# A gated linear attention block on one core: x's statistics, x's low half and the weight splits in another order, and one bank of k's transposes copied by VectorE

## The chip, the cores and the metric

The kernel runs on one core of a Trainium2 chip. The metric is the device time of one execution in microseconds (us), as a median of several runs; lower is better.

## The reference

Four sequences of 2048 tokens of 512 elements pass through two residual layers, all in float32:

```python
q = elu(LN(x) @ Wq) + 1;  k = elu(LN(x) @ Wk) + 1;  v = LN(x) @ Wv      # 16 heads of 64
a = sigmoid(LN(x) @ Wa + ba + 2.0)                                       # one decay per token and head
S = a * S + k (outer) v;   z = a * z + k                                 # for each head, token by token
x = x + ((q @ S) / (q @ z + 1e-6)) @ Wo
x = x + (LN(x) @ CB.T) * (SCB / 127) + bias
```

## The kernel before

The 8192 tokens are 64 chunks of 128 (NC = 64). The first phase computes the projections and the recurrence and stores the attention's rows in memory; the second phase (`step2`) applies Wo and the second layer. The change is in the first phase alone.

Every engine runs its own program: `steps` calls `step(i, pair, b)` for each chunk i, with pair = i // 2 and b = i % 2. Steps -1 to 3 and 60 to 65 are written out, those between are a loop over pairs. The order within an engine is the order of the calls in `step`, written by hand; between engines there are only semaphores, whose counts are values like "16 per load and pair" (`counts` gives a table: `x16[d]` is 16 (pair + d + 1)). A wait blocks everything behind it on its engine.

x is kept transposed for two chunks at a time (`xT_in`) and is split into a high and a low half, `xT_hi` by ScalarE and `xT_lo` by VectorE; each product is three passes, high by high, high by low and low by high. The weights are split in the same way, once, at the start: `split_hi(n)` and `split_lo(n)`, in six slabs n in the order of `order`, each when its load has landed and before the unit that needs it.

A step of TensorE begins with small matmuls: `transposes` of k into the two banks of SC, the carried part of the attention (`carried`), the state's update (`delta`, into DS), the part within a chunk (`within`) and the `scores` (into SC again, once k's transposes have been copied to `kT`). Group r = 1 is the upper half of the heads and runs one chunk behind group 0. Then come the units: products of 12 matmuls of 512 columns (k1, v1, k0, v0) and of 24 of 256 (q units). In a step with b = 1 the order is k1, v1, k0, q0, q1, v0, and `gate_logits` for the next pair runs before `within(0)`; with b = 0 it is k1, v1, q2, q3, k0, v0. k0, v0, q0 and q1 belong to the next chunk or pair.

VectorE has the elementwise work of both groups: `weighted_v`, `state`, `normalised`, `masked`, `scaled_q`, the sums `elu_k` and `elu_q`, the scans of `decay_matrix`, and for a pair `logit_sums`, `decays` and the statistics of x (`x_stats`, `x_moments`). ScalarE evacuates the banks. GpSimd raises the variance to the power -1/2 and normalises `xT_in` for the next pair (`x4`, L593 and L597) after SyncE has spread the moments over the partitions through memory (`spread_norm`).

SyncE issues all DMAs. In a step with b = 1 its order is: spread the decays of group 1, store attn of group 1, `store_decays` (waits for `decays()`), spread the decays of group 0, spread the products, store attn of group 0, and last `load_pair`, which is this (L461 to L466):

```python
for s in range(2):
    later = row(sp, i + 3 + s)
    sp.wait_ge(stats_ready, pairs[1])
    ...
    sp.dma_start(xt[s][:, :], x_rows[bass.ds(later, C), :]).then_inc(x_loaded[s], 16)
```

xt holds the rows of which `x_stats` takes the statistics. Pair 0's rows are loaded at the start, those of pair p + 2 in the step with b = 1 of pair p. In the kernel before, the step with b = 0 of pair p reads the rows of pair p + 1.

Of the kernel before, what the change touches and what calls it, by code (L numbers as in the profile page):

```python
# [5 lines left out]
def gated_linear_attention_block(  # L6
# [50 lines left out]
    GH = 4  # L57
# [59 lines left out]
    with ExitStack() as ctx:  # L117
# [498 lines left out]
        def _(act):  # L616
# [14 lines left out]
            for s in range(2):  # L631
                first_x_hi(s)

# [17 lines left out]
            def step(i, pair, b):  # L651
# [75 lines left out]
                if exists(i) or exists(i - 1):  # L727
                    copy_kT()
                if exists(i - 2):
                    copy_num(1)  # L730
                if exists(i - 1):
                    copy_num(0)
                if b == 1 and exists(i + 1):
                    exp_logits()
                    if not first:
                        act.wait_ge(xT_normal, pairs[0])
                        act.wait_ge(v_unit_ready[1], one[-1])
                        act.wait_ge(q_unit_ready[3], pairs[0])
                        x_hi(0)
                if second:  # L740
                    split_hi(3)
                if exists(i):
                    k1_parts()
                    if second:
                        split_hi(4)
                    copy_v(1)
                if b == 1:
                    if exists(i + 1):
                        if not first:
                            x_hi(1)  # L750
                        k0_parts()
                        if first:
                            split_hi(1)
                        q_parts(0)
                        if first:
                            split_hi(2)
                        chunk_decay()
                        q_parts(1)
                        copy_v(0)
                    elif exists(i):  # L760
                        chunk_decay()
                        rows_hi(1, 0)
                elif exists(i):
                    if second:
                        split_hi(5)
                    q_parts(2)
                    chunk_decay()
                    q_parts(3)
                    k0_parts()
                    copy_v(0)  # L770
# [21 lines left out]
        def _(dve):  # L792
# [50 lines left out]
            for s in range(2):  # L843
                x_lo(s, 1, tiles_of(xT_bank(s)))

# [41 lines left out]
            def step(i, pair, b):  # L887
                one = counts(dve, i, 1, (-3, -2, -1, 0, 1))
                pairs = counts(dve, pair, 1, (-1, 0, 1))
                x16 = counts(dve, pair, 16, (-1, 1))  # L890
# [124 lines left out]
                if gates:  # L1015
                    logit_sums()
# [5 lines left out]
                if gates:  # L1022
                    decays()
                    if not first:
                        x_lo(0, pairs[1], xT_in[:, :, tokens(0)])
                if normal:
                    x_stats(x16[1])
                if exists(i - 1):
                    if normal:
                        dve.wait_ge(stats_ready, pairs[1])  # L1030
                        wait(dve, norm_stored, x16[-1])
                    normalised(0)
                elif normal:
                    dve.wait_ge(stats_ready, pairs[1])
                if normal:
                    x_moments(pairs[1])
                if isinstance(i, int) and i == NC - 1:
                    output_weights_lo(1)
                if second:
                    split_lo(3)  # L1040
                if exists(i):
                    elu_k(1, 0)
                    if second:
                        split_lo(4)
                    if gates:
                        x_lo(1, pairs[1], xT_in[:, :, tokens(1)])
                    decay_matrix(1)
                    weighted_v(1, one[0], one[-1], o)
                if gates:
                    elu_k(0, 1)  # L1050
                    if first:
                        split_lo(1)
                    elu_q(0, 0)
                    if first:
                        split_lo(2)
                    elu_q(1, 1)
                elif exists(i + 1):
                    if second:
                        split_lo(5)
                    elu_q(2, 1)  # L1060
                    elu_q(3, 0)
                    elu_k(0, 1)
                if exists(i + 1):
                    decay_matrix(0)
# [39 lines left out]
        def _(pe):  # L1104
# [52 lines left out]
            first_due = {"k transposed": FIRST + 1, "gates": FIRST // 2 + 1}  # L1157
            for r in range(2):
                first_due[f"carried{r}"] = FIRST - r
                first_due[f"within{r}"] = FIRST - r  # L1160
                first_due[f"delta{r}"] = FIRST + 1 - r
                first_due[f"scores{r}"] = FIRST + 1
# [7 lines left out]
            def step(i, pair, b):  # L1170
# [66 lines left out]
                def carried(r):  # L1237

                    count = due(f"carried{r}", one[-1 - r])
                    pe.wait_ge(qs_ready[r], one[-1 - r])  # L1240
                    if r == 1:
                        wait(pe, num_copied[0], one[-2])
                    elif exists(i - 2):
                        pe.wait_ge(num_copied[1], one[-2])
                    pe.wait_ge(mid_ready[r], count)
                    begin(f"carried{r}")
                    for j in range(GH):
                        for e in range(2):
                            for a in range(2):
                                ps = slice(64 * e, 64 * e + 64)  # L1250
                                made = nc.tensor.matmul(num_of(a, e, j), qs[ps, GH * r + j, L * a:L * a + L],
                                                        (S_mid if a else S[o])[ps, GH * r + j, :],
                                                        start=(j == 0), stop=False)
                    made.then_inc(inter_ready[r], 1)

                def within(r):

                    count = due(f"within{r}", one[-1 - r])
                    pe.wait_ge(M_ready[r], one[-1 - r])
# [11 lines left out]
                def delta(r):  # L1271

                    count = due(f"delta{r}", one[0 - r])
                    if r == 1:
                        wait(pe, state_ready[0], one[-1])
                        if b == 0 and exists(i + 1):
                            pe.wait_ge(logits_ready, pairs[0])
                    elif exists(i - 1):
                        pe.wait_ge(state_ready[1], one[-1])
                    pe.wait_ge(vw_ready[r], count)  # L1280
                    begin(f"delta{r}")
# [10 lines left out]
                def scores():  # L1292

                    for r in (1, 0):
                        if exists(i - r):
                            count = due(f"scores{r}", one[0])
                            for u in range(2 * r, 2 * r + 2):
                                pe.wait_ge(q_ready[u], pairs[-1] if r == 1 and b == 0 else pairs[0])
                            pe.wait_ge(kT_copied[0], one[0])
                            pe.wait_ge(kT_copied[1], count)  # L1300
                            begin(f"scores{r}")
# [74 lines left out]
                if b == 1 and exists(i + 1):  # L1376
                    gate_logits()
# [6 lines left out]
                if b == 1 and exists(i + 1):  # L1384
                    k0_unit()
                    wait(pe, v_ready[1], one[0])
# [93 lines left out]
```

## Time and profile before

| | |
|---|---|
| time, median of 3 runs | 2191.49 us (2190.68 to 2196.81) |
| the profiled execution's own time | 2204.02 us |
| its span | 2202.2 us |
| TensorE matmuls (PE) | 2064.2 us, 94% |
| TensorE weight loads (PEld) | 1773.7 us, 81% |
| VectorE (DVE) | 1497.7 us, 68% |
| ScalarE (ACT) | 677.4 us, 31% |
| GpSimd (POOL) | 340.1 us, 15% |
| mean granted clock of TensorE | 0.988 |

The weight loads overlap the matmuls. A busy TensorE is not one at its peak: the ends of pipelined matmuls are modelled, so a start-to-start distance says more than a duration. The first phase takes about the first 1450 us. Times in the rows are from the span's start.

### The profile page before, as it was taken

To read this page: it belongs to the slowest core of one execution; us is meant where nothing else is said; L and a number is where in the kernel's file an instruction comes from. 1 tells how busy PE (TensorE), PEld (TensorE's weight loads), DVE (VectorE), ACT (ScalarE), POOL (GpSimd) and SP (SyncE) were. 2 spreads that over 40 slices of the span, in tenths; PEclk is the share of its full clock that TensorE was granted. 3 is DMA by queue.
4 is the path that set the end of the run, shared out by engine and by line. 5 is a ranking of instruction groups with operands and counts; after the bars stand their busy time and mean duration, and the time that the engine had idled before them with its cause. 6 is when DMAs were issued, how large, how long until landed. Compare 5 with 4: busy or idle time off the path is not lost. (4 is left out here: it accounts for less than half of the span.)

```text
span 2202.2 us, 71551 instructions
## 1 busy us (share of the span) xinstructions
PE 2064.2 (94%) x28424; PEld 1773.7 (81%) x28424; DVE 1497.7 (68%) x3308; ACT 677.4 (31%) x1288; POOL 340.1 (15%) x367
## 2 busy tenths in 40 slices
PE   4789999999999999999999999999889999999998
PEld 3677888888888888888888888888768888888887
DVE  5566767777767777777776777776755555555555
ACT  3333333333333333333333333333321111111111
POOL 1111122111113111112211112211000000000000
PEclk8899999999999999999999999999999999999999
DMA  5132332333332333333233333324423333333332
GB/s 178 43 95 84 96 96 82 87 98 113 94 94 86 86 91 107 100 96 91 86 85 105 108 91 96 86 82 131 124 99 114 114 114 111 113 114 111 111 110 88
DMA packets 204592, 220.81 MB, mean 100 GB/s; under 512 B 31360, under 2 KB 146560, under 8 KB 204544
## 3 DMA queue, kind: packets, MB, share of 16 engines
q1 hardware_dynamic: 204544, 220.13, 32.7%
q8 instruction: 35, 0.57, 0.1%
q14 instruction: 13, 0.11, 0.0%
HBM read 168.59 MB, written 51.44 MB: 100 GB/s over the span
## 5 line engine op out<-in xcount | busy, mean ns | idle before, releaser
L1189 PE MATMUL G<-w_hi,xT_hi 128*128 128x512 f32 x1024 | 414.2, 404 | 55.2 <-DVE xT_lo L817 39.2
L1189 PE MATMUL G<-w_lo,xT_hi 128*128 128x512 f32 x1024 | 404.0, 395 | 0.0
L1189 PE MATMUL G<-w_hi,xT_lo 128*128 128x512 f32 x1024 | 401.9, 392 | 0.0
L1189 PE MATMUL G<-xT_hi,w_hi 128*128 128x256 f32 x1024 | 292.0, 285 | 8.3 <-DVE w_lo L824 8.3
L1189 PE MATMUL G<-xT_hi,w_lo 128*128 128x256 f32 x1024 | 292.0, 285 | 0.0
L1189 PE MATMUL G<-xT_lo,w_hi 128*128 128x256 f32 x1024 | 291.9, 285 | 0.0
L681 ACT ACTIVATE relu_t<-G 128x512 f32<-128x512 f32 x256 | 152.8, 597 | 450.7 <-PE G L1189 450.7
L1189 PEld LDWEIGHTS G<-w_hi,xT_hi 128*128 128x128 f32 x1024 | 194.6, 190 | 109.5 <-issue 68.5
L906 DVE SCALAR_TENSOR_TENSOR qT<-exp_t,relu_t 128x512 f32<-128x512 f32 x128 | 88.9, 695 | 257.3 <-ACT exp_t L682 257.3
L1189 PEld LDWEIGHTS G<-w_hi,xT_lo 128*128 128x128 f32 x1024 | 194.6, 190 | 42.8
L1189 PEld LDWEIGHTS G<-w_lo,xT_hi 128*128 128x128 f32 x1024 | 195.0, 190 | 35.3
L1146 PE MATMUL DS<-w_hi 128*128 128x512 f32 x512 | 207.7, 406 | 6.3 <-DVE w_lo L861 6.3
L1189 PEld LDWEIGHTS G<-xT_hi,w_hi 128*128 128x128 f32 x1024 | 198.7, 194 | 11.6 <-issue 9.2
L1146 PE MATMUL DS<-w_lo,w_hi 128*128 128x512 f32 x512 | 200.9, 392 | 0.0
L1189 PEld LDWEIGHTS G<-xT_hi,w_lo 128*128 128x128 f32 x1024 | 198.7, 194 | 2.4
L1146 PE MATMUL DS<-w_hi,w_lo 128*128 128x512 f32 x512 | 200.2, 391 | 0.0
L1189 PEld LDWEIGHTS G<-xT_lo,w_hi 128*128 128x128 f32 x1024 | 198.6, 194 | 0.0
L578 POOL TENSOR_TENSOR moments<-vareps,minus_half 128x2 f32<-128x2 f32 x32 | 33.7, 1052 | 1031.7 <-DVE vareps L805 1031.7
L785 ACT ACTIVATE w_hi<-SC 128x512 fp32r<-128x512 f32 x64 | 38.3, 599 | 494.8 <-PE SC L1134 494.8
L999 DVE TENSOR_TENSOR_SCAN D<-abc,eye 128x512 f32<-128x512 f32 x128 | 176.5, 1379 | 0.0
L593 POOL TENSOR_TENSOR xT_in<-xT_in,bias_b 128x256 f32<-128x256 f32 x124 | 137.4, 1141 | 190.3 <-DMA bias_b<-norm_rows 190.3
L670 ACT ACTIVATE num_sb<-NUM 128x520 f32<-128x520 f32 x128 | 77.4, 605 | 251.1 <-PE NUM L1266 251.1
(131 smaller groups left out, 3757.2 us busy)
## 6 DMA issues: line engine op xcount, KB each, us to landing
abc<-decay_rows SPq DMA_DIRECT2D x256, 128.0 KB, 3.0
pbc<-product_rows SPq DMA_DIRECT2D x256, 128.0 KB, 3.1
attn_rows<-attn SPq DMA_DIRECT2D x512, 64.0 KB, 2.0
at_rows<-attn_rows SPq DMA_DIRECT2D x64, 512.0 KB, 3.3
xt<-in_x SPq DMA_DIRECT2D x64, 256.0 KB, 2.7
x_in<-in_x SPq DMA_DIRECT2D x64, 256.0 KB, 3.4
out_rows<-xt SPq DMA_DIRECT2D x64, 256.0 KB, 2.0
xT_in<-in_xT SPq DMA_DIRECT2D x31, 512.0 KB
```

The costliest lines, as they stand in the source:

```text
L578: pool.tensor_tensor(moments[:, :, 1], vareps[:, :], minus_half[:, :], ALU.pow).then_inc(rstd_ready, 1)
L593: made = pool.tensor_tensor(x4[:, kt, :, :], x4[:, kt, :, :], norm_b[:, 0, :, :], ALU.subtract)
L670: act.activation(num_sb[r][:, :, :, :], num_banks, ACT.Copy).then_inc(num_copied[r], 1)
L681: act.activation(relu_t[buffer][:, :], bank[:, :], ACT.Relu)
L785: act.activation(by_stretch(fT_hi), both_of(TF), ACT.Copy).then_inc(fT_hi_ready, 1)
L906: nc.vector.scalar_tensor_tensor(qT[:, QT * u:QT * u + QT, :].rearrange("p k c -> p (k c)"), exp_t[buffer][:, :], 1.0, relu_t[buffer][:, : ...
L999: nc.vector.tensor_tensor_scan(D[:, hs(r), :].rearrange("p h c -> p (h c)"), abc[:, HH * L * r:HH * L * (r + 1)], eye8[:, :, :].rearrange( ...
L1146: made = nc.tensor.matmul(to, a[:, kt, :], w[:, kt, :], start=(kt == 0 and n == 0), stop=(kt == tiles_k - 1 and n == 2))
L1189: made = nc.tensor.matmul(to, lhs, rhs, start=(n == 0), stop=(n == len(passes) - 1))
```

## The change

- Splits: slab 1 is split right behind slab 0, and slabs 2 to 5 each one place earlier in the first two steps.
- ScalarE copies only the first bank of k's transposes; VectorE copies the second as the first thing in its step.
- ScalarE: for the next pair, `x_hi(0)` goes ahead of `copy_num(0)`, and `exp_logits` behind it.
- VectorE, b = 1: `x_lo(0)` goes ahead of `decays()`; `decay_matrix(0)` ahead of `elu_q(1, 1)`; `x_stats` and `x_moments` move here from the step with b = 0, and read the rows of pair p + 2. With b = 0, `decay_matrix(0)` goes ahead of `elu_q(3, 0)`. The second pair's statistics (step 0) go behind `elu_q(2, 1)`.
- TensorE: waits of `carried`, `within`, `delta(1)` and `scores` are gathered ahead of `transposes`, and `scores` waits once for both groups. In step -1 `gate_logits` follows the first k unit.
- SyncE's and GpSimd's programs are as before.

```diff
 split_hi(0)
 for s in range(2):
     first_x_hi(s)
+split_hi(1)
...
-                    for a in range(2):
-                        act.activation(kT[:, held, stretch(a)], turned_k[a][:, held, :], ACT.Copy)\
-                            .then_inc(kT_copied[a], 1)
+                    act.activation(kT[:, held, stretch(0)], turned_k[0][:, held, :], ACT.Copy).then_inc(kT_copied[0], 1)
...
+                if gates and not first:
+                    act.wait_ge(xT_normal, pairs[0])
+                    act.wait_ge(v_unit_ready[1], one[-1])
+                    act.wait_ge(q_unit_ready[3], pairs[0])
+                    x_hi(0)
                 if exists(i - 1):
                     copy_num(0)
-                if b == 1 and exists(i + 1):
+                if second:
+                    split_hi(4)
+                if gates and not first:
                     exp_logits()
...
-                normal = b == 0 and exists(i + 2)
-
+                normal = b == 1 and exists(i + 3) and not first
+
+                if exists(i) or exists(i - 1):
+                    held = slice(0 if exists(i) else GH, PT if exists(i - 1) else GH)
+                    dve.wait_ge(kT_ready, one[0])
+                    nc.vector.tensor_scalar(kT[:, held, stretch(1)], turned_k[1][:, held, :], 1.0, None, ALU.mult)\
+                        .then_inc(kT_copied[1], 1)
...
-                if gates:
+                if gates and not first:
+                    x_lo(0, pairs[1], xT_in[:, :, tokens(0)])
                     decays()
-                    if not first:
-                        x_lo(0, pairs[1], xT_in[:, :, tokens(0)])
-                if normal:
-                    x_stats(x16[1])
...
                     elu_q(0, 0)
                     if first:
-                        split_lo(2)
+                        split_lo(3)
+                    decay_matrix(0)
+                    if normal:
+                        x_stats(x16[2])
+                        dve.wait_ge(stats_ready, pairs[2])
+                        dve.wait_ge(norm_stored, x16[0])
                     elu_q(1, 1)
+                    if normal:
+                        x_moments(pairs[2])
                 elif exists(i + 1):
+                    elu_q(2, 1)
+                    decay_matrix(0)
                     if second:
-                        split_lo(5)
-                    elu_q(2, 1)
+                        x_stats(x16[1])
+                        dve.wait_ge(stats_ready, pairs[1])
                     elu_q(3, 0)
+                    if second:
+                        x_moments(pairs[1])
                     elu_k(0, 1)
-                if exists(i + 1):
-                    decay_matrix(0)
...
                 def transposes():
 
                     count = due("k transposed", one[0])
+                    for r in range(2):
+                        if exists(i - 1 - r):
+                            pe.wait_ge(M_ready[r], one[-1 - r])
+                            pe.wait_ge(qs_ready[r], one[-1 - r])
+                            pe.wait_ge(mid_ready[r], one[-1 - r])
                     if exists(i - 1):
+                        pe.wait_ge(vw_ready[1], one[-1])
+                        pe.wait_ge(state_ready[0], one[-1])
+                        wait(pe, num_copied[0], one[-2])
+                        if b == 0 and exists(i + 1):
+                            pe.wait_ge(logits_ready, pairs[0])
+                        for u in range(2, 4):
+                            pe.wait_ge(q_ready[u], pairs[-1] if b == 0 else pairs[0])
                         pe.wait_ge(k_ready[1], one[-1])
-                        wait(pe, M_ready[1], one[-2])
                     if exists(i):
-                        wait(pe, M_ready[0], one[-1])
+                        pe.wait_ge(q_ready[0], pairs[0])
                         pe.wait_ge(k_ready[0], count)
...
                 def scores():
 
+                    count = due("scores", one[0])
+                    if exists(i):
+                        pe.wait_ge(q_ready[1], pairs[0])
+                    pe.wait_ge(kT_copied[0], one[0])
+                    pe.wait_ge(kT_copied[1], count)
+                    begin("scores")
```

## Rows read from the trace of the kernel before

**Rows 1.** The page: TensorE's and VectorE's busy time, and the granted clock in 40 slices.
```profile
PE 2064.2 (94%) x28424; PEld 1773.7 (81%) x28424; DVE 1497.7 (68%) x3308; ACT 677.4 (31%) x1288; POOL 340.1 (15%) x367
...
PEclk8899999999999999999999999999999999999999
```

**Rows 2.** The waits of TensorE in the loop, 235 to 1374 us: total, times, longest.
```profile
PE G L1189 <- DVE xT_lo L817: 31.4, 24, 1.3
PE DS L1328 <- POOL xT_in L597: 14.5, 16, 2.2
PE DS L1287 <- DVE S L934: 7.4, 17, 0.6
```

**Rows 3.** TensorE in order of time, one pair: start us, us, instruction, idle before.
```profile
711.04 0.71 PE L1134 MATMUL SC<-ident,k 64*128 64x64 f32 x16
...
715.63 0.70 PE L1287 MATMUL DS<-vw,k 64*64 64x65 f32 x32 [0.60 <-DVE S L934]
...
724.88 0.47 PE L1189 MATMUL G<-w_hi,xT_hi 128*128 128x512 f32 x1 [1.31 <-DVE xT_lo L817]
...
736.29 0.71 PE L1134 MATMUL SC<-ident,k 64*128 64x64 f32 x16
...
738.55 1.25 PE L1308 MATMUL SC<-qT,kT 64*64 64x64 f32 x64
...
740.12 0.70 PE L1287 MATMUL DS<-vw,k 64*64 64x65 f32 x32
...
741.22 0.50 PE L1189 MATMUL G<-w_hi,xT_hi 128*128 128x512 f32 x1
...
758.14 0.71 PE L1134 MATMUL SC<-ident,k 64*128 64x64 f32 x16
```

**Rows 4.** VectorE in order of time, the same pair.
```profile
710.72 1.88 DVE L999 TENSOR_TENSOR_SCAN D<-abc,eye 128x512 f32<-128x512 f32 x1
...
724.07 0.06 DVE L992 MEMSET aT<- 128x2 f32 x1
...
735.46 0.69 DVE L906 SCALAR_TENSOR_TENSOR qT<-exp_t,relu_t 128x512 f32<-128x512 f32 x1 [2.88 <-ACT exp_t L682]
736.07 1.22 DVE L999 TENSOR_TENSOR_SCAN D<-abc,eye 128x512 f32<-128x512 f32 x1
737.38 0.70 DVE L915 TENSOR_TENSOR vw<-v,D 128x520 f32<-128x520 f32 x1
...
739.09 0.86 DVE L934 SCALAR_TENSOR_TENSOR S<-S_mid,pc,DS 128x65 f32<-128x65 f32 x4
...
745.05 1.28 DVE L796 BATCH_NORM_STATS2 stats<-xt 128x6 f32<-128x512 f32 x2
...
747.48 0.24 DVE L802 BATCH_NORM_AGGREGATE moments<-stats 128x2 f32<-128x6 f32 x2
```

**Rows 5.** The start: TensorE's waits for the weights' low halves, and VectorE in order of time.
```profile
PE G L1189 <- DVE w_lo L824: 24.4, 5, 7.8
...
8.76 0.69 DVE L840 TENSOR_SCALAR xT_in<-SC 128x512 f32<-128x512 f32 x1 [1.27 <-PE SC L1109]
...
75.29 0.69 DVE L906 SCALAR_TENSOR_TENSOR qT<-exp_t,relu_t 128x512 f32<-128x512 f32 x1 [6.76 <-ACT exp_t L682]
```

**Rows 6.** SyncE's issues in order of time, the same pair.
```profile
724.31 0.36 SPq L453 DMA_DIRECT2D decay_rows<-aT  x1
...
734.82 1.02 SPq L466 DMA_DIRECT2D xt<-in_x  x2
```

**Rows 7.** The page: DMA issues of xt, KB each, us to landing.
```profile
xt<-in_x SPq DMA_DIRECT2D x64, 256.0 KB, 2.7
```

**Rows 8.** GpSimd in order of time, the end of the normalisation.
```profile
758.64 4.59 POOL L597 TENSOR_TENSOR xT_in<-xT_in,bias_b 128x256 f32<-128x256 f32 x4
```

**Rows 9.** Stretches around a long wait: busy us by engine, then the granted clock.
```profile
111.60:114.60 3.00, 0.21 (x16) 0.07 (x6) 1.30 (x3) 0.00 (x0) 0.00 (x0) 1.00 0.36 97
...
115.50:118.90 3.40, 3.40 (x16) 2.71 (x9) 3.11 (x11) 0.60 (x1) 0.00 (x0) 0.50 0.09 24
```

More of the change, by code:

```diff
@@ L728, in step @@
                     copy_kT()
+                gates = b == 1 and exists(i + 1)
                 if exists(i - 2):
                     copy_num(1)
+                if gates and not first:
[3 more added lines that the diff above has]
+                    x_hi(0)
                 if exists(i - 1):
                     copy_num(0)
-                if b == 1 and exists(i + 1):
+                if second:
+                    split_hi(4)
+                if gates and not first:
                     exp_logits()
-                    if not first:
[L736 to L741, printed above, removed]
                 if exists(i):
@@ L744, in step @@
                     if second:
-                        split_hi(4)
+                        split_hi(5)
                     copy_v(1)
-                if b == 1:
-                    if exists(i + 1):
[L749 to L762, printed above, removed]
+                if gates:
+                    if not first:
+                        x_hi(1)
+                    k0_parts()
+                    if first:
+                        split_hi(2)
+                        exp_logits()
+                    q_parts(0)
+                    if first:
+                        split_hi(3)
+                    chunk_decay()
+                    q_parts(1)
+                    copy_v(0)
+                elif b == 1 and exists(i):
+                    chunk_decay()
+                    rows_hi(1, 0)
                 elif exists(i):
-                    if second:
-                        split_hi(5)
                     q_parts(2)
@@ L888, in step @@
                 one = counts(dve, i, 1, (-3, -2, -1, 0, 1))
-                pairs = counts(dve, pair, 1, (-1, 0, 1))
-                x16 = counts(dve, pair, 16, (-1, 1))
+                pairs = counts(dve, pair, 1, (-1, 0, 1, 2))
+                x16 = counts(dve, pair, 16, (-1, 0, 1, 2))
                 c32 = counts(dve, i, 32, (-1, 0, 1))
@@ L1021, in step @@
                         scaled_q(r)
-                if gates:
+                if gates and not first:
+                    x_lo(0, pairs[1], xT_in[:, :, tokens(0)])
                     decays()
-                    if not first:
-                        x_lo(0, pairs[1], xT_in[:, :, tokens(0)])
-                if normal:
-                    x_stats(x16[1])
                 if exists(i - 1):
-                    if normal:
-                        dve.wait_ge(stats_ready, pairs[1])
-                        wait(dve, norm_stored, x16[-1])
                     normalised(0)
[L1033 to L1036, printed above, removed]
                 if isinstance(i, int) and i == NC - 1:
@@ L1039, in step @@
                 if second:
-                    split_lo(3)
+                    split_lo(4)
                 if exists(i):
                     elu_k(1, 0)
-                    if second:
-                        split_lo(4)
                     if gates:
@@ L1051, in step @@
                     if first:
[L1052 removed]
+                        logit_sums()
+                        split_lo(2)
+                        decays()
                     elu_q(0, 0)
                     if first:
[L1055 removed]
+                        split_lo(3)
[4 more added lines that the diff above has]
+                        dve.wait_ge(norm_stored, x16[0])
                     elu_q(1, 1)
+                    if normal:
+                        x_moments(pairs[2])
                 elif exists(i + 1):
+                    elu_q(2, 1)
+                    decay_matrix(0)
                     if second:
[L1059 to L1060 removed]
+                        x_stats(x16[1])
+                        dve.wait_ge(stats_ready, pairs[1])
                     elu_q(3, 0)
+                    if second:
+                        x_moments(pairs[1])
                     elu_k(0, 1)
[L1063 to L1064 removed]
                 if isinstance(i, int) and i == NC - 3:
@@ L1155, in output_product @@
                     made.then_inc(Y_ready, 1)
[L1157 to L1162, printed above, removed]
+            first_due = {"k transposed": FIRST + 1, "within1": FIRST - 1, "scores": FIRST + 1, "carried": FIRST - 1,
+                         "delta": FIRST + 1, "gates": FIRST // 2 + 1, "within0": FIRST}
             due_of = {stage: pe.alloc_register(stage.replace(" ", "_") + "_due") for stage in first_due}
@@ L1237, in carried @@
                 def carried(r):
[L1239 to L1246, printed above, removed]
+                    if not (exists(i) or exists(i - 1)):
+                        pe.wait_ge(M_ready[r], one[-1 - r])
+                        pe.wait_ge(qs_ready[r], one[-1 - r])
+                        pe.wait_ge(mid_ready[r], one[-1 - r])
+                        pe.wait_ge(num_copied[0], one[-2])
+                    if r == 0 and exists(i - 2):
+                        count = due("carried", one[-2])
+                        pe.wait_ge(num_copied[1], count)
+                        begin("carried")
                     for j in range(GH):
@@ L1271, in delta @@
                 def delta(r):
[L1273 to L1281, printed above, removed]
+                    if r == 0:
+                        count = due("delta", one[0])
+                        if exists(i - 1):
+                            pe.wait_ge(state_ready[1], one[-1])
+                        pe.wait_ge(vw_ready[0], count)
+                        begin("delta")
                     for j in range(GH):
@@ L1292, in scores @@
                 def scores():
+                    count = due("scores", one[0])
[4 more added lines that the diff above has]
+                    begin("scores")
                     for r in (1, 0):
                         if exists(i - r):
[L1296 to L1301, printed above, removed]
                             for j in range(GH):
@@ L1375, in step @@
                     delta(0)
-                if b == 1 and exists(i + 1):
+                if b == 1 and exists(i + 1) and exists(i):
                     gate_logits()
@@ L1385, in step @@
                     k0_unit()
+                    if not exists(i):
+                        gate_logits()
                     wait(pe, v_ready[1], one[0])
```

8 lines of the change are left out of this document (5 added, 3 removed).

## The prediction, made before the kernel was timed

> **What bounds the kernel now.** I read the page first, then the waits of the loop, then one pair of chunks in order of time on TensorE, VectorE and SyncE. The page [rows 1] shows TensorE busy for 2064 of 2202 us at its full clock but for the first slices: the kernel is TensorE's queue, and only its gaps can be won. The waits of 24 loop pairs (235 to 1374 us) [rows 2] name three repeating gaps: the low half of x, `xT_lo`, ahead of k's first unit of the next chunk (31.4 us, 24 times 1.3), the pair's normalised x for the gate logits (14.5 us) and the state that frees DS for `delta(0)` (7.4 us). Over the 30-odd pairs of the kernel that is about 1.3 + 0.6 + 0.3 = 2.2 us a pair, some 70 us: the most that the reordering could win in the loop.
>
> In the pair in order of time [rows 3] the odd step (b = 1) begins with its transposes at 711.04, the even step with those at 736.29, and the next pair at 758.14: 47.10 us. This pair has the `xT_lo` gap (724.88) and a `delta(0)` gap of 0.60, and no gap before the gates; with the mean waits of [rows 2] an average pair is 47.1 + 0.6 (gates) - 0.3 (its delta is above the mean) = 47.4 us. All offsets below are from the transposes of b = 1.
>
> **What the change takes away.** `x_lo(0)` goes ahead of `decays()`, and `x_hi(0)` ahead of the copy of NUM. Today `decays()` ends at 724.07 with xT_lo just behind [rows 3, 4]; moving it saves the chain of reciprocal and scans, 2.0 us, against a gap of 1.3: the gap goes. `decay_matrix(0)` leaves the end of the step; in this pair it ran 1.88 us at 710.72 beside GpSimd's work (1.22 us at 736.07 without it) [rows 4], so the state of group 1 comes about 0.6 us sooner even with the added copy of kT. That copy is not in the trace on VectorE; the nearest row is its copy of one PSUM bank into SBUF, 0.69 us [rows 5]. I take 0.65 from start to start. It costs VectorE 0.65 x 64 = 42 us; its floor on TensorE is zero, for ScalarE's second copy no longer follows the first, and scores starts when both banks are copied. The state loses 0.65 and gains the scan: nothing of the 0.60 of `delta(0)` left is my low bound, all of it my high one; I take 0.3.
>
> The waits gathered ahead of the transposes concern values made one step before. At most seven pairs of semaphores are read there, and TensorE's queue reaches them while the last unit's matmuls run. I cost them at nothing; k's first half is the last awaited, and nothing is queued behind it but the transposes. Uncovered they would add some tenths of a microsecond to each step, 0 to 20 us in all.
>
> **What it adds: a wait on a load that is issued too late.** `x_stats` moves from the even step of pair p+1 to the odd step of pair p, between `decay_matrix(0)` and `elu_q(1, 1)`, and it now reads `x16[2]`: 16 (p + 3). That count is reached only by the load that SyncE issues in `load_pair()` of this same odd step, and SyncE's program is not in the diff. Today the statistics run at 745.05 [rows 4], about seven microseconds after those rows have landed. Now the landing counts:
> - `decays()` ends at offset 13.1 (724.07 + 0.06 - 711.04). In the new order it has `x_lo(0)` (0.6) and the copy (0.65) ahead of it and loses the slow scan and the 0.6 of `delta(0)`; I keep 13.1 (12.3 to 14.0).
> - SyncE stores the decays at 724.31 and then issues in its order the spreads of decays and products, four stores of attn, and xt at 734.82 to 735.84 [rows 6]. Its order is not changed: two issues take 1.02 us, so the second begins about 0.65 after the first, 11.4 after `decays()`. With 2.7 us to landing [rows 7] it is there at 13.1 + 11.4 + 2.7 = 27.2. Today `elu_q(1, 1)` starts at 735.46, offset 24.4.
> - From there VectorE is one chain: the second statistics 0.7, `elu_q(1, 1)` 0.6, `x_moments` 0.4 (0.27 and the small add), then the copy of kT's second bank 0.65, so scores can start at 29.7 instead of 738.55, offset 27.5 [rows 3, 4]. `scores()` waits for exactly these two, `q_ready[1]` and `kT_copied[1]`. TensorE, early by the 2.2 us of gaps that it lost, wants scores at 27.5 - 2.2 = 25.3. It idles 4.4 us.
> - Behind the copy stand `weighted_v(0)` and `state(1)`: from the start of vw (737.38) to the end of S (739.95) are 2.6 us [rows 4], and `delta(0)` waits for that: 29.6 + 2.6 = 32.2. From `delta(0)` to the first unit are 1.1 (740.12 to 741.22), and from there to the next pair 16.9 (758.14) [rows 3]. The pair is 32.2 + 1.1 + 16.9 = 50.2 us, against 47.4: **+2.8 us**. What is late next: qs of the even step and with it SyncE's products and the norm. They shift with the step, and GpSimd's normalisation ends about 5 us into the next odd step as it does today (758.64 + 4.59) [rows 8], where the gates begin; a remaining wait of 0 to 0.6 is in the bounds.
> - The clock. In the first pairs TensorE stood for 3.0 us (111.6 to 114.6), and in the 3.4 us from 115.5 the granted clock was 0.50, 1.2 GHz [rows 9]; that gave 3.4 us of matmuls at half speed, 1.6 us lost. Waits of 1.3 us in the loop leave the clock whole. An idle stretch of 4.4 us in every pair lies above the 3.0 that dropped it. Here 3.6 us of small matmuls and a second wait stand between the gap and the units, and part of the slow stretch falls there. I take 1.2 us a pair, between nothing and two such stretches, 3.2.
>
> The Trainium skill ("TensorE: Matmul & The Clock Gate", Part 1: The HAM clock gate) says that the half clock is the default and that activity releases it. By that rule a wait of this length is paid twice; with it the time is the 2302 below, without it 2266.
>
> Loop sum: (2.8 + 1.2) x 30 = +120 us (the statistics run at b = 1 in 30 steps, i = 1 to 59). The last two pairs have no such wait and only gain: -3.
>
> **The start.** Five waits for weight halves cost 24.4 us of TensorE [rows 5]. Splits now go one place ahead, at once behind the first: the second, fourth and fifth waits should shrink, which I put at -13. Against it the statistics of the second pair move from the middle of step 0 to behind `elu_q(2, 1)`, which is now at 75.29 [rows 5]. From moments at 747.48 to the end of the normalisation at 763.2 are 15.8 us [rows 4, 8], and the gates of the first odd step come sooner than that after `elu_q(2)`: some 7 us of wait. Net -6, between -20 and +8.
>
> **Sum.** 120 - 3 - 6 = +111 us on the profiled execution's own 2204.0, so 2315; that execution lies 12.5 above the median of the runs, 2191.49, and the same difference gives **2302 us**.
>
> **The rivals.**
> 1. *The load's wait without the clock* (0.20). The same wait, but the drop falls over the small matmuls: 2.8 x 30 - 9 = +75, 2266. For it: the units start 3.6 us after the gap. Against: the wait of 3.0 us was followed by the low clock [rows 9], and this one is longer.
> 2. *The load is hidden, and the reordering pays: faster* (0.10). Were xt there before offset 23.1, `elu_q(1, 1)` would start with ScalarE's exponentials at 24.4 as today; then scores at 24.4 + 0.6 + 0.4 + 0.65 = 26.1, the pair 26.1 + 2.6 + 1.1 + 16.9 = 46.7, 0.7 less than now: -21 - 9 = -30, **2161**. It decides at a landing at 24.4 (50.2 less 2.8 is 47.4), 2.8 us before the one worked out. Against it: 11.4 us of issues, each about half a microsecond, stand between decays and load.
> 3. *No change* (0.03): the landing falls between, within 6 us of 2191.5.
> 4. *Worse* (part of the likeliest): every pair pays two slow stretches and the gates wait too: (2.8 + 3.2 + 0.6) x 30 - 9 = +189, 2380. It needs all bounds at once.
>
> **How the numbers follow.** The likeliest (the wait with a clock drop) holds 0.67, its own range 2270 to 2345. A difference of 0.3%, 6.6 us, is about what a measurement of this kernel can tell from none. Slower 0.87, same 0.03, faster 0.10. The range leaves out the faster rival and the worst: 2235 to 2345, its low end the first rival with landings half a microsecond sooner (-15) and the start at -20.
>
> **What the changed profile would show.** Right: VectorE's statistics released by the DMA of xt, some 5 us thirty times; SC's scores behind VectorE's kT with gaps over 4 us; no wait on xT_lo; a pair of 50 to 52 us; granted clock under 1 in slices all through the first 1500 us; weight waits under 24 us. Wrong: statistics with no wait before them, and scores at 25 to 26. The prediction fails if SyncE reaches the load sooner than 11 us after the decays, or if the clock stays at full through the gap.

## The result, and the profile after

The changed kernel takes **2311.74 us** (2311.08 to 2316.86, 4 runs); the kernel before took 2191.14 us (2190.68 to 2196.81, 4 runs) beside it. The ratio is 1.0549, 95% interval 1.0526 to 1.0572: **slower by 5.5%**, 120.6 us. The forecast was 2302 in a range of 2235 to 2345, with 2270 to 2345 as the likeliest case's own.

The page answers to [rows 1]. TensorE's busy time hardly grew, from 2064.2 to 2088.2 us, while the span grew by 107 (the profiled execution of the kernel before ran 12.5 us above its median). The clock row shows a 9 in both pages and hides what happened: the mean granted clock fell from 0.988 to 0.965. The last row, the landing of xt after its issue, is as in [rows 7].

```profile
span 2309.3 us, 71079 instructions
...
PE 2088.2 (90%) x28424; PEld 1798.9 (78%) x28424; DVE 1490.8 (65%) x3373; ACT 648.2 (28%) x1223; POOL 302.8 (13%) x367
...
PEclk9999999999999999999999999999989999999999
...
xt<-in_x SPq DMA_DIRECT2D x64, 256.0 KB, 2.8
```

The waits of TensorE over nearly the same stretch as [rows 2] (235 to 1370 us): in total, times, longest.

```profile
PE SC L1318 <- DVE kT L1009: 95.1, 22, 5.0
PE G L1191 <- DVE xT_lo L816: 20.0, 22, 0.9
```

One wait is new and it is the largest: the scores for VectorE's copy of k, once in every pair, 4.3 us on average in the loop. The gap before the gates is gone from the list.

VectorE's list over the whole execution shows who holds that copy up, and a second thing that the kernel before did not have: idle time ahead of the copy with no releaser shown ("issue").

```profile
DVE stats L795 <- DMA xt<-in_x: 152.0, 44, 5.4
...
DVE kT L1009 <- issue: 21.5, 28, 0.8
```

TensorE in order of time for one pair, as in [rows 3]: start, us, instruction, idle before.

```profile
692.55 0.71 PE L1140 MATMUL SC<-ident,k 64*128 64x64 f32 x16
...
708.12 0.36 PE L1191 MATMUL G<-xT_hi,w_hi 128*128 128x256 f32 x1 [0.92 <-DVE xT_lo L816]
...
716.78 0.71 PE L1140 MATMUL SC<-ident,k 64*128 64x64 f32 x16
...
723.27 1.36 PE L1318 MATMUL SC<-qT,kT 64*64 64x64 f32 x64 [4.22 <-DVE kT L1009]
...
727.38 0.54 PE L1191 MATMUL G<-w_hi,xT_hi 128*128 128x512 f32 x1
...
744.30 0.71 PE L1140 MATMUL SC<-ident,k 64*128 64x64 f32 x16
```

This pair lasts 744.30 - 692.55 = 51.75 us, against 47.10 in [rows 3] and a forecast of 50 to 52. VectorE and SyncE in the same pair, as in [rows 4] and [rows 6]:

```profile
705.59 0.06 DVE L992 MEMSET aT<- 128x2 f32 x1
...
707.29 0.68 DVE L816 TENSOR_TENSOR xT_lo<-xT_in,xT_hi 128x512 fp32r<-128x512 f32 x1
...
719.04 1.44 DVE L795 BATCH_NORM_STATS2 stats<-xt 128x6 f32<-128x512 f32 x2 [4.83 <-DMA xt<-in_x]
720.51 0.69 DVE L906 SCALAR_TENSOR_TENSOR qT<-exp_t,relu_t 128x512 f32<-128x512 f32 x1
...
721.40 0.17 DVE L804 TENSOR_SCALAR vareps<-moments 128x2 f32<-128x2 f32 x1
722.34 0.69 DVE L1009 TENSOR_SCALAR kT<-SC 128x512 f32<-128x512 f32 x1 [0.78 <-issue]
```

```profile
705.83 0.36 SPq L453 DMA_DIRECT2D decay_rows<-aT  x1
...
716.34 1.02 SPq L466 DMA_DIRECT2D xt<-in_x  x2
```

Read from the bottom: SyncE stores the decays at 705.83 and reaches the rows of x at 716.34, 10.5 us later, as in [rows 6]. The statistics wait 4.83 us for their landing; `elu_q(1, 1)`, the moments and the copy of k follow one behind the other; the copy starts at 722.34 and the scores at 723.27. Offsets from the odd transposes: decays done 13.1 (forecast 13.1), scores 30.7 (forecast 29.7). Between the moments and the copy stand 0.78 us in which VectorE waits for nothing that the profile shows. One pass of the loop, an even and an odd step, ends there.

Around the gap the granted clock, to be read beside [rows 9] (busy us by engine, then the clock): whole inside the idle stretch, 0.77 in the 6.8 us behind it, whole again after.

```profile
719.05:723.27 4.22, 0.00 (x1) 0.03 (x1) 3.32 (x8) 0.60 (x1) 0.69 (x1) 1.00 0.79 252
...
724.30:731.10 6.80, 6.80 (x126) 5.97 (x120) 5.99 (x21) 1.24 (x3) 0.00 (x0) 0.77 0.15 39
731.10:744.00 12.90, 12.90 (x82) 11.61 (x80) 7.04 (x11) 4.43 (x9) 3.22 (x4) 1.00 0.39 102
```

At the start, for [rows 5], the waits for weight halves ahead of the units (0 to 140 us) fell from 24.4 to 2.5 us and the gates of the first odd step wait once for the late normalisation.

```profile
PE DS L1338 <- POOL xT_in L597: 5.8, 1, 5.8
PE G L1191 <- DVE w_lo L823: 2.5, 2, 1.8
```

### The profile page after: what moved, and what is told of

The parts are those of the page before. It is cut to its first block and busy times, and to the rows that moved or that the text cites. A ratio compares the mean times of both kernels' runs of the same rounds, so it can differ in the third digit from the quotient of the medians.

```text
span 2309.3 us, 71079 instructions
## 1 busy us (share of the span) xinstructions
PE 2088.2 (90%) x28424; PEld 1798.9 (78%) x28424; DVE 1490.8 (65%) x3373; ACT 648.2 (28%) x1223; POOL 302.8 (13%) x367
## 5 line engine op out<-in xcount | busy, mean ns | idle before, releaser
L1318 PE MATMUL SC<-qT,kT 64*64 64x64 f32 x4096 | 94.4, 255 | 140.5 <-DVE kT L1009 137.7
L1318 PEld LDWEIGHTS SC<-qT,kT 64*64 64x64 f32 x4096 | 85.9, 166 | 144.5 <-issue 136.3
L593 POOL TENSOR_TENSOR xT_in<-xT_in,bias_b 128x256 f32<-128x256 f32 x124 | 119.5, 995 | 556.8 <-DMA bias_b<-norm_rows 556.8
```

The lines of the kernel that those rows point to most:

```text
L593: made = pool.tensor_tensor(x4[:, kt, :, :], x4[:, kt, :, :], norm_b[:, 0, :, :], ALU.subtract)
L1318: made = nc.tensor.matmul(SC[64 * a:64 * a + 64, at:at + L], kT[ps, GH * r + j, ts], qT[ps, GH * r + j, C * (b ^ r) + L * a:C * (b ^ r) + ...
```

## The experiments

Ratios are to the kernel before, run on the same chip as the version. It took 2191.1 us beside the changed kernel, 2192.5 beside experiments 1 to 4, 2188.5 beside 5 to 8 and 2198.2 beside 9 to 11. Differences between versions of different groups are of medians, and good to some 5 us, with the last group to some 10.

**1. The statistics back in the even step.** The rest of the change stays.

```
-                normal = b == 1 and exists(i + 3) and not first
+                normal = b == 0 and exists(i + 2)
...
+                if normal:
+                    x_stats(x16[1])
+                if exists(i - 1):
+                    if normal:
+                        dve.wait_ge(stats_ready, pairs[1])
...
+                    x_moments(pairs[1])
```

> The changed kernel, but x_stats and x_moments stand again in the even step and read the load of the odd step before. Theory (the late load is the whole loss): the wait on xt is gone, scores start about offset 25 to 26, a pair takes 46.5 to 47, and the time is 2150 to 2175 us, below the kernel before. Rival (the gathered waits on TensorE or VectorE's copy cost the time): the time stays above 2230 us.

Measured: 2157.16 us (2154.89 to 2159.9), ratio 0.984 [0.9819, 0.9862]. No wait for k's copy is left in the loop (235 to 1370 us):

```profile
PE G L1189 <- DVE xT_lo L816: 22.0, 24, 0.9
PE DS L1295 <- DVE S L934: 18.8, 40, 0.8
```

So the move of the statistics costs 2312 - 2157 = 155 us, and all the rest of the change gains 34.

**2. The statistics where the change has them, the load early.** SyncE issues the rows of x at the head of the odd step.

```
+                if b == 1 and exists(i + 3):
+                    load_rows()
                 if exists(i):
                     spread_decays(1, this)
```

> The changed kernel with its statistics where the change puts them, but SyncE issues the two loads of xt as the first thing of the odd step instead of the last. Theory: the rows land some 20 us before they are read, the wait on xt is gone and the time is 2150 to 2175 us. Rival (it is the place of the statistics in VectorE's order, not the load): over 2230 us. If the bank copy or the gathered waits cost it, also over 2230.

Measured: 2186.33 us (2182.99 to 2191.75, 10 runs), ratio 0.9975 [0.9962, 0.9987]. The late rows account for 2312 - 2186 = 125 of the 155 us. The 2150 to 2175 were missed by 11 us: 29 us over experiment 1 remain although no DMA holds the statistics. In order of time 7 of them lie ahead of the transposes of step 5 (at 168.82 us, in experiment 1 at 162.02), where the second pair's statistics are late, and 22 in the 28 pairs from there to step 61 (1329.0 against 1307.3 us), 0.8 a pair. The waits of the loop, TensorE's and then VectorE's:

```profile
PE DS L1302 <- DVE S L939: 23.4, 42, 0.8
...
PE SC L1323 <- DVE kT L1014: 14.2, 24, 1.1
```

```profile
DVE qT L911 <- issue: 36.0, 24, 2.0
...
DVE kT L1014 <- issue: 18.7, 24, 0.8
```

The first row is a wait for ScalarE's exponential, though no releaser is shown: in one pair the statistics are over at 713.80, the exponential ends at 715.03, and `elu_q(1, 1)` starts at 715.22. So the statistics themselves hold up nothing here. What stands ahead of the copy that releases the scores are the moments and the 0.8 us at the end of the loop's pass, in all 24 pairs. From the start of `elu_q(1, 1)` to that of the copy are 1.83 us here (715.22 to 717.05), in experiment 1 0.94, and that is about what a pair lost:

```profile
698.44 0.69 DVE L906 SCALAR_TENSOR_TENSOR qT<-exp_t,relu_t 128x512 f32<-128x512 f32 x1 [2.54 <-ACT exp_t L681]
699.38 0.69 DVE L1009 TENSOR_SCALAR kT<-SC 128x512 f32<-128x512 f32 x1 [0.24 <-PE SC L1138]
```

Even in time, the moments are in a worse place.

**3. The statistics alone.** The kernel before, with nothing changed but their place.

```
-                normal = b == 0 and exists(i + 2)
+                normal = second
+                late = b == 1 and exists(i + 3) and not first
...
+                    if late:
+                        x_stats(x16[2])
+                        dve.wait_ge(stats_ready, pairs[2])
+                        dve.wait_ge(norm_stored, x16[0])
                     elu_q(1, 1)
+                    if late:
+                        x_moments(pairs[2])
```

> The kernel before with one part of the change alone: the statistics in the odd step ahead of elu_q(1, 1), reading the load of the same step. Theory: scores wait till 28.6 and the state of group 1 till 32.8, since the scan of group 0 stands behind it; a pair of 50.9 us and 30 times 3.5 us give about 2296 us, 2330 with a slow clock behind the second wait. Rival (the loss needs the whole reordering): within 20 us of 2191.

Measured: 2337.5 us (2334.09 to 2338.99), ratio 1.0661 [1.0639, 1.0683]: one part of the change alone loses 146 us, 7 above the top of what was expected. TensorE's waits in the loop are for S and, with no releaser shown, before the scores; VectorE's is for the same rows of x.

```profile
PE DS L1294 <- DVE S L934: 64.1, 37, 2.8
...
PE SC L1315 <- issue: 15.3, 22, 1.2
```

```profile
DVE stats L796 <- DMA xt<-in_x: 110.6, 27, 5.1
```

**4. The load ahead of the four stores of attn only.** These are 2.9 us of issues, about the 2.8 us by which rival 2's deciding point and the forecast were apart.

```
+                if b == 1 and exists(i + 3):
+                    load_rows()
                 if exists(i - 1):
                     store_rows(0, i - 1, one[-1])
```

> The changed kernel, with the two loads of xt issued ahead of the four stores of attn of group 0 instead of behind them, 2.9 us sooner. Theory with the clock: the wait shrinks by 2.9 us and with an idle stretch of about 1.5 us the clock stays whole, so 30 times 4.1 to 4.4 us come back: 2180 to 2190 us. Theory without the clock: 30 times 2.9, 2225 us. Rival (not the load): 2312, unchanged.

Measured: 2220.86 us (2216.98 to 2224.35), ratio 1.0128 [1.0107, 1.0149]. The waits of the loop for the copy of k fall from 95.1 to 42.4 us and those of the statistics for the rows are still there:

```profile
PE SC L1323 <- DVE kT L1014: 42.4, 23, 2.6
```

```profile
DVE stats L800 <- DMA xt<-in_x: 61.3, 25, 3.4
```

91 us for 2.9 us of issues, 30 times: 3.0 us a pair. The load is issued 2.9 us sooner, but now takes longer to land, 3.3 us against the 2.8 of the changed kernel:

```profile
xt<-in_x SPq DMA_DIRECT2D x64, 256.0 KB, 3.3
```

So the rows are there 2.4 us sooner, and the wait for the copy of k shrinks by as much, from 4.3 to 1.8 us a time. What is left of the 3.0 us a pair goes to the clock by this account, which came back: 0.985 in the profiled execution, against 0.965. The time is that of the expectation without the clock, but for another reason: less of the wait went than 2.9 us, and the clock did play a part. The time is still 29 us above the kernel before.

**5. What is left of the gap for xT_lo.** Experiment 1, with the low half of the pair's second row directly behind `decays()`.

```
                     x_lo(0, pairs[1], xT_in[:, :, tokens(0)])
                     decays()
+                    x_lo(1, pairs[1], xT_in[:, :, tokens(1)])
...
-                    if gates:
-                        x_lo(1, pairs[1], xT_in[:, :, tokens(1)])
                     decay_matrix(1)
```

> As e1_stats_back, with x_lo(1) moved ahead of normalised(0) and elu_k(1, 0), right behind decays(). If the 0.9 us that TensorE still waits for xT_lo in each pair of e1 comes from x_lo(1) standing behind those four instructions, it goes, and the time is about 2157 - 31 x 0.9 = 2130 us. If another chain then sets the pair (the spread of the products, which is tied to the decays), little of it comes back: 2145 to 2157.

Measured: 2155.64 us (2152.87 to 2159.14), ratio 0.9844 [0.9827, 0.9861], the same as without. The gap is gone from the loop's waits and comes back one place on:

```profile
PE DS L1294 <- DVE S L934: 25.1, 45, 0.8
PE SC L1315 <- DVE kT L1009: 21.3, 25, 1.0
```

In that step VectorE's `elu_q(1, 1)` waits for ScalarE's exponential, and ScalarE for the products' broadcast by DMA:

```profile
700.65 0.69 DVE L906 SCALAR_TENSOR_TENSOR qT<-exp_t,relu_t 128x512 f32<-128x512 f32 x1 [3.28 <-ACT exp_t L681]
```

```profile
699.41 0.23 ACT L724 ACTIVATE pc<-pbc 128x16 f32<-128x16 f32 x1 [4.61 <-DMA pbc<-product_rows]
```

**6. ScalarE copies both banks again.** Experiment 1 with this one part of the change undone.

```
+                    for a in range(2):
+                        act.activation(kT[:, held, stretch(a)], turned_k[a][:, held, :], ACT.Copy)\
+                            .then_inc(kT_copied[a], 1)
...
-                    nc.vector.tensor_scalar(kT[:, held, stretch(1)], turned_k[1][:, held, :], 1.0, None, ALU.mult)\
-                        .then_inc(kT_copied[1], 1)
```

> As e1_stats_back, but ScalarE copies both banks of k's transposes, as in the kernel before. Forecast of the prediction: the copy on VectorE is worth next to nothing to TensorE; within 10 us of 2157 either way. If it pays (scores start sooner by a copy, 0.5 us in 64 steps), 2185. If it costs (0.65 on VectorE's path to state(1)), 2130 to 2145.

Measured: 2137.37 us (2134.91 to 2141.72), ratio 0.976 [0.9744, 0.9777]. That is 20 us under experiment 7 on the same chip (which differs from experiment 1 in nothing measurable), and beyond both kernels. The waits for S all but vanish:

```profile
PE DS L1292 <- DVE S L936: 0.5, 2, 0.2
```

**7. TensorE's waits not gathered.** Experiment 1 with TensorE's whole program as it was before.

> As e1_stats_back, with TensorE's whole program as in the kernel before: each stage waits for itself, nothing is gathered ahead of the transposes. Forecast of the prediction: no cost and no gain, within 6 us of 2157. Rival (fewer waits between the small stages save time at each of them): 0.1 to 0.3 us a step, 2164 to 2176. Rival (waits ahead of the transposes cost): 2145.

Measured: 2157.56 us (2156.76 to 2161.21), ratio 0.9857 [0.9838, 0.9876]. Gathering the waits neither costs nor gains.

**8. The gap filled.** The changed kernel; in each even step TensorE repeats twelve matmuls of the next unit, whose result is written over, where it would stand idle. Their time lies inside the wait.

```
+                if b == 0 and exists(i) and exists(i - 2):
+                    pe.wait_ge(exp_q_ready[1], pairs[0])
+                    product(G0[:, :], [(xp[:, kt, tokens(b)], w[:, NP + 1, kt, :]) for kt, xp, w in parts])
                 if exists(i) or exists(i - 1):
                     scores()
```

> The changed kernel, with twelve more matmuls in each even step between within(1) and scores: k's first unit of that step is computed once more into the same bank, to be written again by the real one. They take 2.7 us of the 4.4 us that TensorE idles, and VectorE's chain is as before. Theory (the idle stretch lowers the clock, 1.2 us a pair): the granted clock goes back to about 0.99 and the time falls by some 30 us to 2280. Rival (the clock plays no part): 2312, or more if the added matmuls cost.

Measured: 2290.61 us (2289.78 to 2293.16), ratio 1.046 [1.0442, 1.0479]: more work, and 21 us less time, where 30 had been expected. In order of time the gain in the loop is larger: the 28 pairs from the odd transposes of step 5 to those of step 61 take 1429.5 us here (169.25 to 1598.78) and 1456.4 in the changed kernel, 0.97 less each. Part of it is lost again where the twelve are done and no gap is to be filled: from step 61 to step 63 are 54.4 us here and 49.6 in the changed kernel. From the scores to the first unit are 714.43 - 711.17 = 3.26 us here, 727.38 - 723.27 = 4.11 in the changed kernel; the clock of the stretch, and the scores themselves:

```profile
704.59 0.71 PE L1140 MATMUL SC<-ident,k 64*128 64x64 f32 x16
...
711.17 1.16 PE L1318 MATMUL SC<-qT,kT 64*64 64x64 f32 x64 [1.36 <-DVE kT L1009]
...
714.43 0.50 PE L1191 MATMUL G<-w_hi,xT_hi 128*128 128x512 f32 x1
```

```profile
707.00:718.00 11.00, 9.11 (x188) 7.51 (x188) 9.72 (x31) 1.67 (x4) 0.69 (x1) 1.00 0.36 120
```

The 1.36 us of idle time is what the twelve leave of the gap. From the even step's transposes to the scores are 711.17 - 704.59 = 6.58 us, in the changed kernel 723.27 - 716.78 = 6.49: the scores come no sooner, and only the clock is given back.

**9. Both cures together.** Experiment 6 with experiment 5's move.

> The version with the statistics back in the even step, both banks of k's transposes copied by ScalarE, and the lower half of the second row's x made right behind the decays. With ScalarE's copies alone it took 2137 us and still held 24 waits for that lower half, 0.9 us each (22.0 us). If that wait is all that stands there: 22 us less, 2115 us (2110 to 2122), and no wait of TensorE over 5 us in the loop. Rival: the chain behind it (decays, their broadcast by DMA, ScalarE's scaled parts of q, elu_q) sets the scores now, as it did when the lower half was moved without ScalarE's copy (22 us of waits became 21 us of waits for k's copy and 6 more for S): 2133 to 2141 us, same as without the move.

Measured: 2138.77 us (2135.16 to 2141.99), ratio 0.9729 [0.9716, 0.9742]. The median is that of experiment 6, the ratio 0.3% lower, against a before that ran at 2198 on this chip and at 2189 on the other; which of the two is better is not settled. The waits went as the rival said, from xT_lo to the copy of k:

```profile
PE SC L1312 <- ACT kT L664: 16.3, 24, 0.9
```

**10. The changed kernel, with both copies on ScalarE.**

> The changed kernel, in which ScalarE copies both banks of k's transposes. It tells where the late rows of x strike. Theory: the copy on VectorE stands behind the statistics that wait for the rows, so the scores wait for it (137.7 us of waits in the changed kernel). With the copy on ScalarE the scores are free, but S, which VectorE makes behind the same statistics, is late by the same and delta(0) waits: the loss moves by one place and hardly shrinks. Expected: waits of the scores under 15 us in all, waits of delta(0) for S 80 to 130 us, time 2280 to 2310 us against 2312 for the change. Rival: it is the copy's place on VectorE that costs, and the rest of the step hides the late rows: 2230 us or less, under 60 us of waits for S.

Measured: 2293.77 us (2290.69 to 2295.96), ratio 1.0433 [1.0417, 1.0449]. The time is where it was expected, the waits are not. The scores wait 50.6 us for q, because `elu_q(1, 1)` too stands behind the statistics, which the expectation overlooked, and only 24.0 us are waits for S. Against the changed kernel it is 18 us faster by the medians, 25 by the ratios:

```profile
PE SC L1315 <- DVE qT L908: 50.6, 22, 2.4
PE DS L1294 <- DVE S L936: 24.0, 22, 1.8
```

**11. Only the second pair's statistics late.** Experiment 1, with the one use at the start in the place of the change.

> The version with the statistics back in the even step, except those of the second pair, which stay in the place that the change gave them. It prices the term of the start (gates of the second pair wait for late statistics: +7 us by the prediction). Theory: the gates wait once 5.8 us or so for the rows' transposes as in the changed kernel, and the time is 2157 + 5 to 8 = 2162 to 2165 us. Rival: the wait is paid anyway by another (weights or k's parts in the same stretch), 2157 +- 2 us.

Measured: 2165.87 us (2164.81 to 2170.99), ratio 0.9857 [0.9842, 0.9873]; 8.7 us over experiment 1 by the medians (5 to 8 expected), 3.7 by the ratios. The wait of the start is there:

```profile
PE DS L1341 <- POOL xT_in L597: 6.1, 1, 6.1
```

## Why the prediction was right, point by point

**The late load: right.** `x16[2]` names rows that SyncE loads last in the same step. Undoing the move removes the loss (experiment 1), doing it alone makes the loss (3), moving only the load removes four fifths of it (2), and moving its issue by 2.9 and its landing by 2.4 us gives 3.0 us a pair (4). In size the term was 1.0 us a pair too small: the idle stretch was 4.22 us against 4.4, but the scores started at 30.7, not 29.7. Of that 1.0 us, 0.78 is the idle time of VectorE at the end of the loop's pass, ahead of the copy, which the sum had at nothing.

The traces say more of it. From the start of VectorE's last operation of a pass to the start of its first of the next are 0.94 us in the changed kernel (721.40 to 722.34) and 0.94 in experiment 1 (698.44 to 699.38), though the one ends a pass with the 0.17 us of the moments and the other with the 0.69 of `elu_q(1, 1)`; it is 0.94 or 0.95 in all pairs of both but the first few, and where the profile puts experiment 1's rest down to k's transposes, these had ended before. Where the loop makes no turn there is no such time, as ahead of step 60, with which the written-out steps begin:

```profile
1602.64 0.17 DVE L804 TENSOR_SCALAR vareps<-moments 128x2 f32<-128x2 f32 x1
1602.83 0.69 DVE L1009 TENSOR_SCALAR kT<-SC 128x512 f32<-128x512 f32 x1
```

So it is the loop's turn that takes VectorE 0.94 us, beside its last operation, and what that operation does not cover stays open: 0.78 behind 0.17 us, 0.25 behind 0.69. In the kernel before the last one is a scan of 1.22 us, and the next follows 0.09 behind it [rows 4].

**The clock: right in kind, a little high.** The prediction took 1.2 us a pair. Filling the gap gives back 0.97 us a pair in the loop (8), of which 4.11 - 3.26 = 0.85 lie between the scores and the first unit; 21 us of the whole are left. The Trainium skill ("TensorE: Matmul & The Clock Gate", Part 1: The HAM clock gate) has it that activity releases the full clock; by that rule the repeated matmuls should keep it, and the trace agrees (1.00 through the stretch).

**The gap for xT_lo: half wrong.** The wait for the first row's low half did go. But TensorE then came early to the second row's low half, which `x_lo(1)` makes at 707.29 behind the attn and k of the same step, and waited there 0.9 us in every pair. The step named `xT_lo` as one wait, though two instructions make it. Experiments 5 and 9 show a third chain just behind that one, so the 22 us cannot be had by moving that instruction alone.

**The slow scan: right.** The decay matrices no longer run beside GpSimd: the longest of 128 took 1.22 us, against 1.88 in [rows 4].

**VectorE's copy of k: wrong where the rows are in time.** What it leaves of the gap before `delta(0)` was put at nothing to 0.6 us a pair. In experiment 1 `delta(0)` waited for S 40 times in the loop, and giving the copy back to ScalarE gained 20 us. VectorE is the chain to S, and of the 0.65 x 64 = 42 us of copies about half reached TensorE. The step that failed set the lost 0.65 against the gain of a scan that runs elsewhere; the waits for S grew all the same, from 7.4 us in [rows 2] to 18.8. In the chain of the likeliest case the copy does stand with its 0.65, which makes 20 us in 30 pairs, and there experiment 10's 18 us (25 by the ratios) bear it out.

**The gathered waits: right**, at nothing (7).

**The start: right in sign, low in size.** The same pair of odd transposes starts at 186.48 before and at 168.38 after, 18 us sooner, where -6 had been forecast (within -20 to +8). Two of the 30 steps with late rows lie ahead of this point, which by the forecast's 4.0 us each makes the start better than forecast by some 20. Weight waits fell by 21.9 us, not 13; the gates' late wait cost 4 to 9 us, 7 forecast.

```profile
186.48 0.71 PE L1134 MATMUL SC<-ident,k 64*128 64x64 f32 x16
```

```profile
168.38 0.71 PE L1140 MATMUL SC<-ident,k 64*128 64x64 f32 x16
```

**The sum.** +120.6 us against +111, and that it came so near is in part luck. The two profiled executions are 107 us apart. In them the start is 18 us shorter, and the 28 pairs from step 5 to step 61 take 1456.4 us against 1333.8 (first the kernel before, then the changed one):

```profile
1520.26 0.71 PE L1134 MATMUL SC<-ident,k 64*128 64x64 f32 x16
```

```profile
1624.83 0.71 PE L1140 MATMUL SC<-ident,k 64*128 64x64 f32 x16
```

That is 4.4 us a pair where 4.0 had been forecast; if the 13.5 us by which the medians differ more than these executions lay in the 28 pairs as well, it would be 4.9, and no run tells where they lie. Within a pair the scores came 1.0 us later than forecast, and from them to the next pair were 744.30 - 723.27 = 21.0 us, where 20.5 and 1.2 of the clock had been put. The start's error and that of the loop nearly cancel. By parts, in medians: the reordering with the copy on VectorE -34, the statistics' and moments' new place +29, the late rows +125, of which 20 to 27 by the clock.

**Rival 2** was decided by the wrong point. It made 2191 of a landing 2.8 us sooner and 2161 of one well in time. Measured were 2221 with a landing 2.4 us sooner (the missing 0.4 us would be worth some 12 us, an estimate at 30 pairs) and 2186. It had 1.0 us from the start of `elu_q(1, 1)` to the copy with the moments between; experiment 2 has 1.83, because of the loop's turn.

**Still open:** what VectorE does in the 0.94 us of the loop's turn; no run here tells.

## What to carry to other kernels

When an operation is moved up, read which count its wait names, find the instruction that raises it, and add that engine's queue up to it; a program that is not in the diff can be the one that decides. Then ask again with the data there: experiment 2 shows that work in time can still stand in front of the one instruction that the bottleneck waits for. When an issue is moved up, look at the landing too: 2.9 us became 2.4. Take a change apart before judging it: here one bad move hid 34 us of gain (2191 to 2157), and a second one 20 more (2137).

## What had not been expected of the hardware

- Twelve needless matmuls in each gap made the kernel 21 us faster, by keeping the granted clock at 1.00 where it was 0.77 over 6.8 us.
- Turning the loop takes VectorE 0.94 us from the start of its last operation, and only what this operation does not cover shows: 0.78 us behind one of 0.17, 28 times, 21.5 us in all; 0.25 behind one of 0.69; next to nothing (0.02 us) ahead of step 60, where the loop has ended.
- The same load took 3.3 us to land instead of 2.8 when it was issued right behind the broadcasts of the products instead of behind the stores of attn.
- A fall of the clock did not show inside the idle stretch (1.00 from 719.05 to 723.27) but behind it, as in [rows 9].
